# One transformer block for 800 tokens: feed-forward half in seven packed sets instead of eight padded tiles

## The reference

```
h = patches @ W.T + b                       # 768 -> 256, then the class token in front
h = h + Attn(layernorm(h))                  # 16 heads of 16
    qkv  = x @ Wqkv.T + bqkv                # 256 -> 768
    qkv.reshape(B, 16, 50, 48)              # a head is 50 rows of 48 of an image's flat buffer
    vals = softmax(q @ k.T / 4) @ v ;  vals @ Wo.T + bo
h = h + FFN(layernorm(h))
    relu(x @ w1.T + b1) rounded to a float with 4 exponent and 3 mantissa bits
    @ w2.T (rounded likewise) + b2, rounded to a float with 5 and 10 bits
```

## Time and profile before

| | us |
|---|---|
| median of 3 runs (lowest, highest) | 113.15 (112.34, 114.29) |
| the profiled execution's own time | 112.6 |
| its span, first to last instruction | 110.8 |
| PE busy | 102.9 (93%) |
| PEld busy | 85.7 (77%) |
| DVE busy | 67.2 (61%) |
| POOL busy | 52.1 (47%) |
| ACT busy | 48.4 (44%) |

### The profile page before, as it was taken

One profiled execution on the slowest core, in us unless ns is written; L12 is line 12 of the kernel. 1 busy time (PEld: TensorE's weight loads), 2 busy tenths in 40 slices (PEclk: granted clock), 3 DMA queues, 4 the chain that ended last, 5 costly groups with the idle time before them and its releaser, 6 DMA issues.

```text
span 110.8 us, 3809 instructions
## 1 busy us (share of the span) xinstructions
PE 102.9 (93%) x1532; PEld 85.7 (77%) x1532; DVE 67.2 (61%) x128; ACT 48.4 (44%) x108; POOL 52.1 (47%) x94
## 2 busy tenths in 40 slices
PE   6997999999999979999899999999999999999940
PEld 6786766687767967798798998998897889799830
DVE  5001778595559779489989599688690644410140
ACT  0402110068906861568165347557549263446400
POOL 8791201649967506955938208208323344620040
PEclk9999999999999999999999999999999999999999
DMA  3899997588229415140331130240321002021012
GB/s 81 227 363 401 401 397 265 180 119 314 114 37 290 172 50 103 52 44 10 105 38 49 71 37 30 87 43 13 103 28 12 6 12 62 14 73 32 0 41 70
DMA packets 18785, 12.59 MB, mean 114 GB/s; under 512 B 13968, under 2 KB 15920, under 8 KB 18512
## 3 DMA queue, kind: packets, MB, share of 16 engines
q1 hardware_dynamic: 17868, 11.63, 36.2%
q10 hardware_dynamic: 900, 0.72, 2.2%
HBM read 9.07 MB, written 3.28 MB: 111 GB/s over the span
## 4 chain that ended last, share of the span: by engine, by line
PE 86%; DMA 4%; DVE 2%; issue 2%; SPq 2%; ACT 1%; ACTq 0%
PE psum L377 14%; PE psum L350 8%; PE psum L351 7%; PE psum L352 7%; PE psum L460 7%; PE psum L526 7%; PE psum L579 6%; PE psum L503 6%; PE psum L555 6%; PE psum L483 5%; PE psum L439 5%; DMA x_sb<-in_xt 4%; PE psum L442 3%; PE psum L538 2%; PE psum L406 2%
## 5 line engine op out<-in xcount | busy, mean ns | idle before, releaser
L377 PE MATMUL psum<-x_sb,w_sb 128*128 128x294 f32 (+1 forms) x72 | 18.8, 403 | 0.9 <-DVE qkv_sb L713 0.4
L947 ACT ACTIVATE hq<-psum,cols 128x300 fp8e4<-128x300 f32 (+1 forms) x24 | 11.6, 485 | 17.2 <-PE psum L555 9.1
L1071 POOL TENSOR_SCALAR var_eps<-mv 128x1 f32<-128x1 f32 x16 | 3.6, 225 | 28.4 <-DVE mv L775 16.5
L377 PEld LDWEIGHTS psum<-x_sb,w_sb 128*128 128x128 f32 x72 | 13.2, 201 | 3.9 <-DMA x_sb<-in_xt 1.3
L713 DVE SCALAR_TENSOR_TENSOR qkv_sb<-psum,rstd,bqkv_sb 128x768 f32<-128x768 f32 x8 | 8.1, 1018 | 5.1 <-PE psum L439 2.2
L913 ACT ACTIVATE probs<-shifted 128x400 f32<-128x400 f32 x16 | 7.8, 531 | 7.5 <-DVE shifted L749 7.5
L738 DVE TENSOR_REDUCE rmax<-psum 128x16 f32<-128x800 f32 x8 | 7.9, 982 | 4.7 <-PE psum L460 4.7
L789 DVE TENSOR_TENSOR x_sb<-psum,b_q 128x256 f16<-128x256 f32 x8 | 3.4, 423 | 11.9 <-PE psum L579 11.7
L350 PE MATMUL psum<-xn2T_hi,w_hi 128*128 128x300 f32 x32 | 10.5, 327 | 0.1
L1114 POOL TENSOR_TENSOR vals<-att,rsum 128x256 f32<-128x256 f32 x8 | 4.9, 618 | 10.2 <-DVE rsum L760 10.2
L351 PE MATMUL psum<-xn2T_lo,w_hi 128*128 128x300 f32 x32 | 9.6, 301 | 0.0
(11 more groups left out here) (81 smaller groups left out, 224.3 us busy)
## 6 DMA issues: line engine op xcount, KB each, us to landing
v_rows<-qkv_sb SPq DMA_DIRECT2D x32, 75.0 KB
x_sb<-in_xt SPq DMA_DIRECT2D x6, 294.0 KB, 8.3
w_sb<-in_w1t SPq DMA_DIRECT2D x1, 1024.0 KB, 6.1
w_sb<-in_w2t SPq DMA_DIRECT2D x1, 1024.0 KB, 5.6
v_sb<-v_rows SPq DMA_DIRECT2D x16, 50.0 KB
wqkv_sb<-in_wqkvt SPq DMA_DIRECT2D x2, 384.0 KB, 5.6
wqkv_r<-in_wqkv_rows SPq DMA_DIRECT2D x1, 768.0 KB, 7.4
out<-x_sb SPq DMA_DIRECT2D x26, 25.0 KB
```

The lines of the kernel that those rows point to most:

```text
L377: last = pe.matmul(dst, w_sb[:, k, m * P:(m + 1) * P], x_sb[b][:, k, :], start=(k == 0), stop=(k == KP - 1))
L947: act.activation(hq[:, m, a:b].rearrange("p t j n -> p (t j) n")[:, :, 0:QTOK], p_wide[:, ff1_bank[n], 0:(b - a) * TILE].rearrange("p (q n ...
```

## The change

The second half of the block no longer goes by tiles of 128 partitions with gaps, but by seven sets without gaps: 100, 100, 125, 125, 125, 125 and 100 tokens (`SETS`). `ENDS` names the tile with which each set is complete: 0, 1, 3, 4, 5, 6, 7. `project`, `add_attention`, the second norm, `turn2`, `ff2`, `round_out`, `finish` and the output stores run once for each set. The transposed values (`valsT`), `xn2T` and `hq` are stored without gaps, so the zero fills of `valsT` and `hq` go. The feed-forward batches are sets (0,2), (2,4), (4,7), that is 200, 250 and 350 tokens, and the 24 pieces stand elsewhere in the order: two fewer in the main loop. `qkv(5, 0)` moves from iteration 4 to the end of iteration 3 (`AHEAD`).

The residual must lie as the sets do, so SyncE's queue moves it by DMA within the on-chip memory (`move_tokens`, four DMAs of 25 rows of 1 KB for each tile), issued behind the V load of the tile after, and behind w2's load for the first. VectorE's `add_attention` waits for these. V's store takes only the V columns, in runs of 64 bytes. The output is stored with one DMA for each set, the last with two.

```diff
-FB = [(0, 2), (2, 5), (5, 8)]
+FB = [(0, 2), (2, 4), (4, 7)]
+SETS = [(0, 100), (100, 200), (200, 325), (325, 450), (450, 575), (575, 700), (700, 800)]
+ENDS = [(b - 1) // TILE for a, b in SETS]
...
-        ff1_at = {4: [0], 5: [3], 6: [6], 7: [8, 9, 10, 11]}
-        ff1_mid = {4: [1, 2], 5: [4, 5], 6: [7]}
+        ff1_at = {4: [0], 5: [2], 6: [4], 7: [6, 7, 8, 9]}
+        ff1_mid = {4: [1], 5: [3], 6: [5]}
...
+            def move_tokens(t):
+                sp.wait_ge(h0bo_done, t + 1)
+                for row, d, to in moves(t):
+                    sp.dma_start(h1[to:to + QTOK, d], h0_bo[row:row + QTOK, t]).then_inc(h0_in[d], 16)
...
                 for j in range(QUADS):
-                    sp.dma_start(v_rows[s, j], qkv_sb[32 * j:32 * j + QTOK, s]).then_inc(v_stored, 16)
+                    by_chunk = qkv_sb[32 * j:32 * j + QTOK, s].rearrange("p (c e) -> p c e", e=CHUNK)
+                    sp.dma_start(v_rows[s, j], by_chunk[:, :, 2 * HD:]).then_inc(v_stored, 16)
...
                 elif t == 1:
                     sp.dma_start(w2_sb[:, :, :], w2t).then_inc(w2_in, 16)
...
+                if t >= 1:
+                    move_tokens(t - 1)
+            move_tokens(TILES - 1)
+            last = len(SETS) - 1
+            for d in range(last):
+                sp.wait_ge(out_done, d + 1)
+                store_out(sp, d, 0, size(d))
+            sp.wait_ge(last_done, 1)
+            store_out(sp, last, 0, 64)
...
-            def project(t):
+            def project(d):
+                a, b = SETS[d]
...
-                    last = pe.matmul(p_proj, valsT[:, t % 2, k].rearrange("p j n -> p (j n)"), wo_sb[:, k, :],
+                    last = pe.matmul(psum[0:size(d), 7, 0:D], valsT[:, k, a:b], wo_sb[:, k, :],
...
-                    last = pe.matmul(p_ff2(t), hq[:, k, t].rearrange("p j n -> p (j n)"), w2_q[:, k, :], start=(k == 0), stop=(k == KF - 1))
+                    last = pe.matmul(psum[0:size(d), d % 2, 0:D], hq[:, k, a:b], w2_q[:, k, :], start=(k == 0), stop=(k == KF - 1))
...
-                    qkv(i + 1, 0)
+                    if i + 1 != AHEAD:
+                        qkv(i + 1, 0)
...
-                project(i - 1)
+                if set_ending(i - 1) is not None:
+                    project(set_ending(i - 1))
...
+                if i + 2 == AHEAD:
+                    qkv(AHEAD, 0)
+                if set_ending(i - 2) is not None:
+                    turn2(set_ending(i - 2))
+            ff1(10, TILES)
+            ff1(11, TILES)
+            turn_vals(TILES - 1)
+            ff1(12, TILES)
+            project(6)
+            turn2(5)
+            for n in range(13, 16):
+                ff1(n, TILES)
+            ff2(1, TILES)
+            turn2(6)
+            ff2(2, TILES)
+            ff2(3, TILES)
             for n in range(16, 24):
                 ff1(n, TILES)
+            for d in range(4, 7):
+                ff2(d, TILES)
...
+            def add_attention(d):
+                n = size(d)
+                dve.wait_ge(pe_proj, d + 1)
+                dve.wait_ge(h0_in[d], 16 * moved(d))
+                dve.tensor_tensor(h1[0:n, d], psum[0:n, 7, 0:D], h1[0:n, d], ALU.add).then_inc(h1_done, 1)
...
             add_attention(0)
+            measure2(0)
+            gather2(0)
             for i in range(2, TILES):
...
-                measure2(i - 2)
-                if i + 2 < TILES:
-                    measure1(i + 2)
-                gather2(i - 2)
...
-                add_attention(i - 1)
+                if set_ending(i - 1) is not None:
+                    add_attention(set_ending(i - 1))
+                    measure2(set_ending(i - 1))
+                    gather2(set_ending(i - 1))
...
-            pool.memset(valsT[:, :, :, :, :], 0.0)
...
-            pool.memset(hq[:, :, :, :, :].rearrange("p m t j n -> p (m t j n)").bitcast(F32), 0.0).then_inc(pool_init, 1)
...
-    v_rows = nc.dram_tensor("v_rows", (2, QUADS, QTOK, QKV), F32, kind="Internal").ap()
+    v_rows = nc.dram_tensor("v_rows", (2, QUADS, QTOK, HEADS, HD), F32, kind="Internal").ap()
```

More of the change, by code:

```diff
@@ L60, in cols_of, with set_ending, sets_before, size @@
     return (PB[b][1] - PB[b][0]) * 2 * PATCHES
+def set_ending(t):
+    return ENDS.index(t) if t in ENDS else None
+def sets_before(t):
+    return sum(e < t for e in ENDS)
+def size(d):
+    return SETS[d][1] - SETS[d][0]
+def set_columns(a, b):
+    return SETS[a][0], SETS[b - 1][1]
+def moves(t):
+    found = []
+    for j in range(QUADS):
+        first = t * TILE + j * QTOK
+        d = [n for n, (a, b) in enumerate(SETS) if a <= first < b][0]
+        found.append((32 * j, d, first - SETS[d][0]))
+    return found
+def moved(d):
+    return sum(m[1] == d for t in range(TILES) for m in moves(t))
 def piece(b, c):
@@ L250, in build @@
         h0bo_done = sem("h0bo_done")
+        h0_in = [sem(f"h0_in{d}") for d in range(len(SETS))]
         vals_done = sem("vals_done")
@@ L276, in v_keys, with store_out, all_stored @@
         def v_keys(s, b):
[L277 to L286, removed]
+            return v_rows[s].rearrange("j n c e -> (j n c e)").rearrange("(b u q e) -> b q u e", b=2, q=TOKENS, e=HD)[b]
+        def store_out(queue, d, a, b):
+            queue.dma_start(out[SETS[d][0] + a:SETS[d][0] + b, :],
+                            out_sb[a:b, d % 4]).then_inc(out_stored[d % 4], 16)
+        def all_stored(q):
+            return sum(2 if d == len(SETS) - 1 else 1 for d in range(len(SETS)) if d % 4 == q)
         block = ctx.enter_context(nc.Block())
@@ new lines, in measure2, with gather2, low_turned2 @@
+            def measure2(d):
+                n = size(d)
+                dve.wait_ge(h1_done, d + 1)
+                dve.bn_stats(stats[0:n, 1, d % 2], h1[0:n, d]).then_inc(stats2_done, 1)
+            def gather2(d):
+                n = size(d)
+                dve.wait_ge(stats2_done, d + 1)
+                if d >= 2:
+                    dve.wait_ge(shift2_done, d - 1)
+                dve.bn_aggr(mv[0:n, 1, d % 2], stats[0:n, 1, d % 2]).then_inc(mv2_done, 1)
+            def low_turned2(d):
+                dve.wait_ge(xn2T_hi_done, d - FB[EXACT_FF][1] + 1)
+                part = half_columns(d, d + 1)
+                low(xn2T_h[1][:, :, part], turned2(d), xn2T_h[0][:, :, part].bitcast(F32)).then_inc(xn2T_lo_done, 1)
@@ L826, in _ @@
                     invert(i - 1)
+                if 4 <= i < TILES - 1:
+                    measure1(i + 1)
+                    gather1(i + 1)
                 maxima(i)
@@ L833, in _ @@
                     invert(1)
[L834 to L841 removed]
+                if i == 6:
+                    low_turned2(2)
                 if 3 <= i < TILES - 1:
@@ L846, in _ @@
                     turn_k(i + 1)
[L847 removed]
+                if i == 2:
+                    measure1(4)
+                    gather1(4)
+                if set_ending(i - 1) is not None:
+                    add_attention(set_ending(i - 1))
+                    measure2(set_ending(i - 1))
+                    gather2(set_ending(i - 1))
                 if i == 6:
[L849 to L851 removed]
+                    low_turned2(3)
             turn_att(TILES - 1)
             invert(TILES - 1)
[L854 removed]
+            low_turned2(4)
             round_out(0)
+            add_attention(6)
+            measure2(6)
+            gather2(6)
+            low_turned2(5)
             round_out(1)
[L857 to L860 removed]
+            low_turned2(6)
             round_out(2)
             round_out(3)
[L863 to L869 removed]
+            for d in range(4, 7):
+                round_out(d)
+            d = len(SETS) - 1
+            n = size(d)
+            dve.wait_ge(ff16_done, d + 1)
+            dve.wait_ge(out_stored[d % 4], 16)
+            dve.tensor_tensor(out_sb[0:n, d % 4], ff16[0:n, d % 2], h1[0:n, d], ALU.add).then_inc(last_done, 1)
         @block.scalar
```

266 lines of the change are left out of this document (108 added, 158 removed).

## The result

The changed kernel takes 129.99 us (median of 4, 128.53 to 132.06) against 113.72 (4, 112.34 to 115.04) for the kernel before: 1.142 times as long, 95% interval 1.1332 to 1.1508. Forecast were 111.25, in a range up to 114.3, so the time lies far outside it and on the other side.

What follows compares the result with a forecast made beforehand. PE, busy 102.9 of 110.8 us, was taken as the bound. PE work -1.96, waits +0.3 and tail stores -0.2 gave 108.9, or 111.25 against the median of 113.15; range 109.8 to 114.3.

Steps and rivals of the forecast that it cites:

- V and the moves: SyncE's queue: V's store takes 1.2 to 1.5 us, extra issues and moves are hidden while SP waits; 0 in the sum.
- My slower rival: V's 64-byte stores slow, first moves late: add_attention(0) 3.7 us late, 114.95 us; delays of 1 to 4.5; chance 0.25.
- Attention waits for V 0.2 us in all: Attention's wait for V: taken to mean that a faster V store alone gains nothing; 0.
- same runs, same bytes: V's store priced from V's load at 87 GB/s: 102 KB in 1.2 us, taken as 1.2 to 1.5.
- the share of 0.27 of the engines: DMA engine share of the old 25-row V store, 108 GB/s; evidence for the slower rival, agreeing with 5 engines.
- the bound of five engines at the load's rate: V's new store, if confined to the old store's engines: 3.5 us instead of 2.8.
- The load's 0.94: DMA engine share of V's load from 50 partitions; evidence against the slower rival, as the divisor rule would give 10 engines.
- The PE part: TensorE's work: project -0.88, ff2 -0.88, turn2 -0.2, ff1 0; -1.96 us in sum.
- PE waiting for VectorE: Sign to look for in iteration 4: about 7 us long, VectorE's 7.05 against PE's 6.55, so 0.5 idle.
- The bound I set aside: ff1 on PE: 250 columns take no less than 300 because the weight load sets the pace; +1.1 us, taken as 0.
- what I took back for waits: Waits for ScalarE, of the 0.77 us at 83.27 (iteration 7) and the 0.47 at 53.30: -1.2 us.
- The tail: Output stores behind the last matmul: 125 rows at the same rate, the last 100 KB spread wider; -0.2 us.

Runs made afterwards that it cites:

- b_micro: Kernel before, with single DMAs of seven forms issued on SyncE's queue behind its last store, each waited for; its total time isn't compared.
- packing alone: Changed kernel with V stored by whole rows and without the 32 moves, so wrong residual rows are added; 112.09 us, ratio 0.9939.
- a_nomoves: Changed kernel without the 32 moves, V still stored in 64-byte runs, so wrong tokens are added; 118.45 us, ratio 1.046.
- best3: Changed kernel with V stored by one DMA of 128 rows, four loads, and last output stores cut into 112 + 13 and 64 + 32 + 4 rows; 113.28 us, 0.9882.
- b_runs: Kernel before with only V's store changed, to the V columns in runs of 64 bytes; 118.37 us, ratio 1.0384.
- a_onestore_w2late: Changed kernel with V stored by one DMA of 128 rows, four loads, and w2's load issued behind the moves of tile 2; 113.95 us, ratio 1.0076.

## Why the prediction was wrong

**The failed step** is "V and the moves". It gave the new issues a price ("+0.2 on SP for a tile, and the moves 4 x 0.33 = 1.3 more"), set against it that SP "only waits" between store and load, and so called it hidden. Three things were wrong in it.

First, the prices, by the kernel's profile and by b_micro: V's store 4 x 0.74 = 3.05 with gaps, where 1.5 was assumed; from its last issue to the load 2.6 to 3.2, where the step took 1.2 to 1.5; the moves 2.9 instead of 1.3. The loads are 0.87 as before.

Second, the sum. With the prices of the tile shown it is 3.05 + 3.2 + 0.9 + 2.9 = 10.1 us. In packing alone the engines need 7.0 to 8.2 for one (`scale_qkv` at 50.40, 57.43, 65.13 and 73.29). The moves stand behind the wait and not in it, so the wait hides nothing of them. This could have been seen beforehand: before, from V's store at 51.73 to the load's end at 56.89 is 5.2 us, so 3.5 of 8.7 were free, and of the 7.05 that the prediction left for iteration 4 only 1.9. Even at my own price the moves took 1.3 of these, and at twice my price the queue was over-full, which the range should have asked.

Third, the path. My slower rival named the right suspects, slow 64-byte stores and a late first move, but as one delay of at most 4.5 us at one place. A queue that is too long delays each tile. The first move was late as in that rival: w2 went out at 37.05 instead of 32.29, and VectorE stood 5.03 us, until 43.42, not 3.7. I had the moves landed by 35.7. By that rival's own sum this is 111.25 + 5.0 = 116.3, and the rest is the other tiles.

One more place was taken for free: "Attention waits for V 0.2 us in all" was read as slack. A wait, however short, says that there is none. In a_nomoves this place, tile 1's V, cost 2.8 us of waiting and the clock behind it.

How the 19.9 us between the spans divide: beside packing alone (span 110.4, PE busy 100.5) PE is idle for 23.8 instead of 9.9 us, +13.9, and busy 6.0 longer for the same instructions. Of these 6.0 about 3.5 are the lower clock, worked out from granted means of 0.91 over 45 to 65 and 0.91 over 100 to 119; the rest I did not trace. No term of my sum had a place for the clock, because it was at full speed throughout before. In the other executions it weighs more (5 to 9 us, above).

**What V's stores needed.** I took 1.2 to 1.5 us for landing from V's load, "same runs, same bytes", and left the share of 0.27 of the engines to the rival. With a third of the bytes the wait from the last issue to the load did not shrink: 2.6 to 3.2 us behind 40 us, 2.8 to 3.1 before. The whole way from first issue to load grew from 4.1 to 4.7 us to 5.9 to 6.3, and that is the longer issue. b_micro shows the same for one store. Its data flow for 0.65 us in 25 x 16 runs and for 0.7 in rows of three times the bytes. Of the 0.96 us between the two periods 0.5 is the issue, 0.2 the time from there to the first data and 0.3 that behind the last. So the bound of five engines at the load's rate had the wrong cause. The load's 0.94 was no argument against it either: the profile's share is no count of engines, since it reads 1.09 of 16 for 128 rows over 151.1 to 151.3 us. The Trainium skill, page "DMA: Bandwidth & Descriptors", section "Specifications", says that below 512 bytes a transfer does a read-modify-write. b_micro agrees in that a byte takes nearly three times as long to flow, but no run shows the mechanism.

**The PE part was right.** The calls came out as predicted: ff2, project and turn2 seven times, the tail's three ff2 in 2.73 us. In packing alone iteration 4 is 7.0 us long with VectorE waiting 0.6 for PE in it ("PE waiting for VectorE" was forecast), so VectorE did not become the bound. The bound I set aside, that 250 columns could take as long as 300, is excluded. Packing alone, groups by shape, as in the earlier trace rows:

```profile
L407 PE MATMUL psum<-xn2T_hi,w_lo 128*128 128x350 f32 x16 | 5.2, 323 | 0.0
...
L407 PE MATMUL psum<-xn2T_hi,w_lo 128*128 128x250 f32 x16 | 4.5, 278 | 0.0
```

323 and 278 have a mean of 300.5, which is what 300 columns took, and their slope is 0.45 ns a column, where 0.46 was taken. Mis-sized was what I took back for waits. The last ff2 is done at 105.34 (102.61 + 2.73), where the sum gives 106.55 - 1.96 + 0.3 = 104.9. In iteration 7 turn_probs still waits for ScalarE's two instructions, as long as before:

```profile
80.87 0.33 ACT valsT L997
81.20 0.43 ACT probs L983
```

**The tail was mis-sized.** I said -0.2; from the last ff2 to the end packing alone takes 110.4 - 105.34 = 5.1 us where the kernel before takes 4.25, so +0.8. The stores of 125 rows are slower, not equal. In b_micro 125 rows of 1 KB take 2.53 us from issue to issue and 112 rows 1.86. While the data flow the mean share of the DMA engines is 0.29 for 125 rows, over 1.5 us, and 0.56 to 0.61 for 112, over 0.7 us. The Trainium skill, page "DMA: Bandwidth & Descriptors", section "Why a DMA increments its semaphore by 16 and not by 1", has a DMA use the largest number up to 16 that divides the slowest dimension: 5 engines for 125, 16 for 112. The trace agrees with the direction. With the output cut into 112 + 13 and 64 + 32 + 4, the last ff2 is done at 105.41 and the span ends at 109.2, 3.8 us (best3). The two errors, +0.4 in the middle and +1.0 in the tail, are the 1.5 between 110.4 and the 108.9 of the sum: packing alone gains 0.7 us and not 1.9.

## What to carry to other kernels

For every in-order DMA queue, write down one iteration of it: each issue at the price of its own form, each wait, and what stands behind the wait; if that sum comes near the engines' iteration, nothing put on the queue is free, however idle the DMA engines are. Here a saved byte did not pay for a more fragmented or more frequent DMA: with the moves on the same queue, one store of 384 KB with gaps beat four of 75 KB by 7 us and four of 25 KB in short runs by 17; with room in the queue it was worth nothing. Price a part on the kernel that it goes into: what cost 5.5 and 2.2 us on the old one cost 6.4 and 8.3 on the packed one, and 18 together. And a wait of 0.2 us marks a place without slack, where any delay is paid in full.

## What was not expected of the hardware

- The time that SyncE's queue needs for an issue depends on the form: 0.25 us for 25 rows to DRAM, 0.68 for the same rows within the on-chip memory (0.53 for 32 rows), 0.77 for 25 x 16 runs of 64 bytes to DRAM, 0.55 for 128 x 16 such runs. The count of rows or packets does not explain it (128 x 16 is cheaper than 25 x 16), and why is open.
- A stall can be followed by a stretch at the lower clock: in the change twice, 0.52 to 0.62 granted over some 4 us at full PE load; in a_nomoves 0.50 over 38 to 46 us behind 2.8 us without a matmul; in b_runs 0.50 over 40 to 46 behind 1.8. Not every stall is: in a_onestore_w2late PE works 0.62 of the 2 us at 58 and 1.44 of the next 2, and the clock stays full. In the traced execution of b_runs the clock cost more than the waits for V themselves, 3.2 against 2.2 us.
- A V store in runs needs its time ahead of the data and behind them: 1.4 us pass from its issue to the first data, 0.7 for rows, and then both flow for about 0.7 (b_micro).
- GpSimd can issue the moves at 0.51 us each, and SyncE is free of them; it is GpSimd's own time then.
